# Decoder block on one core: later layernorm rows normalised on GpSimd, query parts in PSUM or on GpSimd, query stack loaded in two sets of heads

## The reference

```python
x = x + self_attention(layernorm(x))              # 16 heads of 64, softmax over the queries' axis
x = x + cross_attention(layernorm(x), ctx, mask)  # q = layernorm(x) @ Wq + bq, 16 heads of 8, 512 keys
x = x + ffn(layernorm(x))                         # softmax gate, best 2 of 8 experts, and a shared expert

def layernorm(x):
    return (x - mean(x)) / sqrt(var(x) + 1e-5)
```

## Time and profile before

| | us |
|---|---|
| median of 3 runs | 215.52 (213.54 to 216.35) |
| the profiled execution | 215.22 |
| its span, first to last instruction | 213.4 |
| PE busy | 198.2 (93%) |
| DVE busy | 160.9 (75%) |
| ACT busy | 131.9 (62%) |
| POOL busy | 91.2 (43%) |

### The profile page before, as it was taken

One profiled execution on the slowest core, in us unless ns is written; L12 is line 12 of the kernel. 1 busy time (PEld: TensorE's weight loads), 2 busy tenths in 40 slices (PEclk: granted clock), 3 DMA queues, 4 the chain that ended last, 5 costly groups with the idle time before them and its releaser, 6 DMA issues.

```text
span 213.4 us, 4411 instructions
## 1 busy us (share of the span) xinstructions
PE 198.2 (93%) x1562; PEld 153.6 (72%) x1562; DVE 160.9 (75%) x421; ACT 131.9 (62%) x308; POOL 91.2 (43%) x133
## 2 busy tenths in 40 slices
PE   7999998999799798697979999999898999999993
PEld 7788776777667575564646566566576899999993
DVE  2578688657659996379999999998994677458752
ACT  2465468669748838168868989988696532362320
POOL 7599017687456566604999700000120003611422
PEclk9999999999999999998899999999999999999999
DMA  6960748999546114024003300000000000000000
GB/s 169 386 172 3 197 49 99 121 108 109 60 57 178 65 30 107 15 60 166 0 0 96 54 3 0 2 3 2 0 3 0 5 0 3 0 0 28 0 0 25
DMA packets 10876, 12.67 MB, mean 59 GB/s; under 512 B 880, under 2 KB 8816, under 8 KB 10784
## 3 DMA queue, kind: packets, MB, share of 16 engines
q1 hardware_dynamic: 10040, 11.28, 26.5%
q10 hardware_dynamic: 720, 0.93, 1.3%
q0 software_dynamic: 96, 0.20, 0.5%
HBM read 10.96 MB, written 1.44 MB: 58 GB/s over the span
## 4 chain that ended last, share of the span: by engine, by line
PE 71%; DVE 17%; issue 5%; ACT 5%; POOL 1%; POOLq 0%; DVEq 0%; ACTq 0%
PE ps L897 12%; PE ps L858 9%; PE ps L918 7%; PE ps L835 6%; PE ps L785 6%; PE ps L674 5%; PE ps L801 5%; PE ps L817 5%; PE ps L757 4%; DVE q_t L1123 4%; PE ps L646 3%; PE ps L687 3%; DVE low L1113 3%; ACT prob L562 2%; PE ps L875 2%
## 5 line engine op out<-in xcount | busy, mean ns | idle before, releaser
L1123 DVE CUSTOM_DVE_ANT_0 q_t<-ps,mask_add 128x512 f32<-128x512 f32 x64 | 41.3, 683 | 5.3 <-PE ps L817 4.0
L457 POOL TENSOR_TENSOR prob<-prob,rec 128x512 f32<-128x512 f32 x32 | 32.7, 1049 | 28.3 <-DVE rec L1176 28.3
L562 ACT ACTIVATE prob<-ps,low 128x256 f32<-128x256 f32 x64 | 29.7, 490 | 11.7 <-DVE low L1113 11.7
L596 ACT ACTIVATE q_t<-q_t,low 128x512 f32<-128x512 f32 x44 | 29.3, 717 | 7.4 <-DVE low L1123 7.4
L392 POOL TENSOR_TENSOR rstd<-var_eps,minus_half 128x2 f32<-128x2 f32 (+1 forms) x5 | 3.9, 773 | 61.0 <-DVE var_eps L984 60.9
L858 PE MATMUL ps<-ident,q_t 128*128 128x128 f32 x176 | 24.1, 278 | 3.9 <-DVE place_o L1219 1.4
L858 PEld LDWEIGHTS ps<-ident,q_t 128*128 128x128 f32 x176 | 20.1, 143 | 10.1 <-issue 4.0
L1113 DVE TENSOR_REDUCE low<-ps 128x2 f32<-128x512 f32 x32 | 20.5, 681 | 7.9 <-PE ps L757 7.9
L582 ACT ACTIVATE q_t<-ps 128x512 f32<-128x512 f32 x18 | 10.6, 599 | 21.0 <-PE ps L897 21.0
L817 PE MATMUL ps<-k_stack,q_stack 72*128 72x512 bf16 x64 | 19.4, 390 | 1.8 <-issue 1.8
L801 PE MATMUL ps<-ident,prob 128*128 128x128 f32 x128 | 18.0, 278 | 2.1 <-DVE prob_t L1180 2.1
(11 more groups left out here) (166 smaller groups left out, 430.3 us busy)
## 6 DMA issues: line engine op xcount, KB each, us to landing
k_stack<-k_dram SPq DMA_DIRECT2D x9, 256.0 KB
q_stack<-q_dram SPq DMA_DIRECT2D x6, 192.0 KB
wg<-in_L_ffn_w_gate SPq DMA_DIRECT2D x1, 1024.0 KB, 24.8
wu<-in_L_ffn_w_up SPq DMA_DIRECT2D x1, 1024.0 KB, 36.1
k_dram<-prob SPq DMA_DIRECT2D x1, 768.0 KB, 3.6
w_in<-in_L_attn_Wq ACTq DMA_DIRECT2D x2, 256.0 KB, 5.6
context<-in_ctx SPq DMA_DIRECT2D x1, 512.0 KB, 5.8
w_in<-in_L_attn_Wv SPq DMA_DIRECT2D x1, 512.0 KB, 7.5
```

Source lines behind the costliest of these rows:

```text
L457: nc.gpsimd.tensor_tensor(pr, pr, rec1[:, s % 2, r, :].unsqueeze(2).to_broadcast([P, C, S]), ALU.mult).then_inc(s_norm1, 1)
L562: e = nc.scalar.activation(prob1[:, s % 3, r, c * S:(c + 1) * S], ps[:, 2 * (s % 2) + r, c * S:(c + 1) * S], ACT.Exp, bias=low1[:, s % 2, ...
L596: nc.scalar.activation(prob2[n % 3][:, c, :], score2[n % 2][:, c, :], ACT.Exp, bias=low2[:, n % 2, c:c + 1], scale=-1.0).then_inc(s_exp2, 1)
L1123: nc.vector.tensor_tensor_reduce(out=score2[n % 2][:, c, :], in0=ps[:, 2 * (n % 2) + c, :], in1=mask_add[:, c, :], scale=1.0, scalar=3e38, ...
```

## The change

- The rows of the four later layernorms (two batches, before cross attention and before the experts) are normalised on GpSimd: adding epsilon, the power and the two `tensor_scalar` operations stand there one behind the other (`normalise`), in the iteration of `residual` and ahead of that iteration's `divide1`. DVE keeps the statistics. The first layernorm stays on DVE.
- DVE makes batch 0's query parts in place in PSUM, and in g = 12 ahead of `reciprocals1(13)`. For batch 1 DVE only adds the bias and scales into SBUF, and GpSimd makes the parts (`split_queries2`) between two of its weight splits.
- The query stack of each batch is loaded in six DMAs: three with heads 0 to 3, then three with heads 4 to 15, and PE waits for each set where its first head comes.

```diff
+QSETS = ((0, 4), (4, H2))
...
-                for j in range(PARTS):
-                    r = j * PARTS * HD2
-                    load(q2_stack[r:r + PARTS * HD2, :, b * S:(b + 1) * S],
-                         q2_dram[b].rearrange("i (d h) t -> (i d) h t", d=HD2), d_qstack[b])
+                rows = q2_dram[b].rearrange("i (d h) t -> (i d) h t", d=HD2)
+                for i, (first, last) in enumerate(QSETS):
+                    for j in range(PARTS):
+                        r = j * PARTS * HD2
+                        load(q2_stack[r:r + PARTS * HD2, first:last, b * S:(b + 1) * S],
+                             rows[:, first:last, :], d_qstack[b][i])
...
+                if k >= 1:
+                    link(nc.gpsimd.tensor_scalar(var_eps[:, first:first + count], mean_var[:, first:first + count, 1],
+                                                 EPS, None, ALU.add))
...
+            def normalise(k, src, first):
+
+                link(reciprocal_std(k, first, C))
+                for c in range(first, first + C):
+                    ins = nc.gpsimd.tensor_scalar(x_hat[:, c, :], src[:, c, :], mean_var[:, c, 0:1],
+                                                  rstd[:, c:c + 1], ALU.subtract, ALU.mult)
+                ins.then_inc(s_xhat, 1)
...
+            def split_queries2():
+
+                pool.wait_ge(s_q2t, 1)
+                pool.wait_ge(d_qdram[0], 16)
+                link(nc.gpsimd.tensor_copy(q2_parts[:, 0, :], q2_t[:, :]))
+                link(nc.gpsimd.tensor_tensor(q2_rest[:, :], q2_t[:, :], q2_parts[:, 0, :], ALU.subtract))
+                link(nc.gpsimd.tensor_copy(q2_parts[:, 1, :], q2_rest[:, :]))
+                nc.gpsimd.tensor_tensor(q2_parts[:, 2, :], q2_rest[:, :], q2_parts[:, 1, :], ALU.subtract
+                                        ).then_inc(s_qparts, 1)
...
             for g in range(LAST_G + 2):
                 n = g - N_SELF
+                for kind, b, _ in BETWEEN.get(g, ()):
+                    if kind == "residual":
+                        normalise(1 + b, x1, b * C)
+                    elif kind == "residual2":
+                        normalise(3 + b, x2, b * C)
                 if g < N_SELF:
                     divide1(g)
...
-                if h == 0:
-                    pe.wait_ge(d_qstack[b], 16 * PARTS)
+                for i, (first, _) in enumerate(QSETS):
+                    if h == first:
+                        pe.wait_ge(d_qstack[b][i], 16 * PARTS)
...
+            def query_parts(b):
+
+                dve.wait_ge(s_q2ps, b + 1)
+                bank = ps[:, MID_BANK, S:2 * S]
+                if b == 1:
+                    nc.vector.tensor_scalar(q2_t[:, :], bank, bias2[:, 0:1], -SCALE2, ALU.add, ALU.mult
+                                            ).then_inc(s_q2t, 1)
+                    return
+                link(nc.vector.tensor_scalar(bank, bank, bias2[:, 0:1], -SCALE2, ALU.add, ALU.mult))
+                link(nc.vector.tensor_copy(q2_parts[:, 0, :], bank))
+                link(nc.vector.tensor_tensor(bank, bank, q2_parts[:, 0, :], ALU.subtract))
+                link(nc.vector.tensor_copy(q2_parts[:, 1, :], bank))
+                nc.vector.tensor_tensor(q2_parts[:, 2, :], bank, q2_parts[:, 1, :], ALU.subtract).then_inc(s_qparts, 1)
...
+                    for what in BETWEEN.get(g, ()):
+                        between(what)
                     reciprocals1(g + 1)
```

More of the change, by code:

```diff
@@ L63 @@
     11: [("residual", 0, 0)],
-    12: [("x_hat", 0, 0), ("turn", 0, 0), ("turned", 0, 0), ("q", 0, 0), ("parts", 0, 0)],
+    12: [("turn", 0, 0), ("turned", 0, 0), ("q", 0, 0), ("parts", 0, 0)],
     N_SELF + 3: [("residual", 1, 0)],
-    N_SELF + 4: [("x_hat", 1, 0)],
     N_SELF + 5: [("turn", 1, 0)],
@@ L74 @@
     N_SELF + 26: [("residual2", 0, 0)],
-    N_SELF + 27: [("x_hat2", 0, 0)],
     N_SELF + 28: [("turn2", 0, 0)],
@@ L293, in build @@
         d_qdram = [sem(f"d_qdram{b}") for b in range(B)]
-        d_qstack = [sem(f"d_qstack{b}") for b in range(B)]
+        d_qstack = [[sem(f"d_qstack{b}_{i}") for i in range(len(QSETS))] for b in range(B)]
         s_const, s_ident = map(sem, ("s_const", "s_ident"))
@@ L391, in reciprocal_std @@
                 pool.wait_ge(s_var, k + 1)
-                nc.gpsimd.tensor_tensor(rstd[:, first:first + count], var_eps[:, first:first + count],
-                                        minus_half[:, first:first + count], ALU.pow).then_inc(s_rstd, 1)
+                if k >= 1:
+                    link(nc.gpsimd.tensor_scalar(var_eps[:, first:first + count], mean_var[:, first:first + count, 1],
+                                                 EPS, None, ALU.add))
+                return nc.gpsimd.tensor_tensor(rstd[:, first:first + count], var_eps[:, first:first + count],
+                                               minus_half[:, first:first + count], ALU.pow)
+            def normalise(k, src, first):
[4 more added lines that the diff above has]
+                ins.then_inc(s_xhat, 1)
             nc.gpsimd.memset(v2[:, :, :, HD2 + 1:CW], 0.0)
@@ L469, in _ @@
                     if kind == "residual":
-                        reciprocal_std(1 + b, b * C, C)
                         add_bo2(b)
-                    elif kind == "residual2":
-                        reciprocal_std(3 + b, b * C, C)
                     elif kind == "turned2":
                         split_tokens(b)
+                    elif kind == "parts" and b == 1:
+                        split_queries2()
                 if 0 <= n - SPLIT_N < 2 * (NE + 1):
                     split_weights(n - SPLIT_N)
-            reciprocal_std(4, C, C)
             for i in range(N_FFN):
@@ L490, in _ @@
                     nc.gpsimd.tensor_tensor(sums, sums, y_part[k % 2], ALU.add).then_inc(s_acc, 1)
+                for kind, row, _ in FFN_BETWEEN.get(i + LAG_D, ()):
+                    if kind == "residual2":
+                        normalise(3 + row, x2, row * C)
         @block.scalar
@@ L985, in statistics @@
                                         EPS, None, ALU.add).then_inc(s_var, 1)
-            def normalise(k, src, first, count):
-                dve.wait_ge(s_rstd, k + 1)
+                dve.wait_ge(s_rstd, 1)
                 for c in range(first, first + count):
@@ L1191, in _ @@
                         low_scores1(g, r)
-                    for what in BETWEEN.get(g, ()):
-                        if what[0] == "x_hat":
-                            between(what)
                     low_scores1(g + 1, 0)
@@ L1213, in _ @@
                     probs_evac(g - 1, 1)
-                for what in BETWEEN.get(g, ()):
-                    if not (cycle(g) and what[0] == "x_hat"):
+                if not (cycle(g) and g < N_SELF):
+                    for what in BETWEEN.get(g, ()):
                         between(what)
```

18 lines of the change are left out of this document (5 added, 13 removed).

## The result

| | before | changed |
|---|---|---|
| median, us (4 runs each) | 214.97 (213.54 to 216.35) | 208.0 (207.6 to 208.76) |
| span of the profiled execution | 213.4 | 206.1 |
| PE, DVE, ACT, POOL busy | 198.2, 160.9, 131.9, 91.2 | 195.5, 153.2, 132.1, 100.2 |

The ratio is 0.968 (95% interval 0.961 to 0.975): 7.0 us less, where 5.3 were forecast. The ratios in this document leave out executions more than 1.5% above the fastest of their kernel; medians and ranges hold all of them.

The account below looks back on a forecast made before the run. PE was taken to set the end nearly everywhere. Terms 1.3 + 1.8 + 1.8 + 0.4 = 5.3 us off the profiled 215.22 gave 209.9, own range 208.8 to 211.0, whole range 207.5 to 213.0.

Parts of the forecast that it names:

- The wait before the first score: Between self and cross attention: loading queries in two sets hides PE's hole before the first cross score, 1.8 us.
- The entry without the hole: End of self attention: earlier, shorter query parts of batch 0 in PSUM let PE's transposes of pair 13 start earlier, 1.3 us.
- the bound of 0.73: Batch 0's layernorm on POOL: upper limit for one normalising operation, the time of a two-input operation twice as wide.
- Cost nothing, but the cover is thin: End of self attention: pair 11's divisions, queued behind POOL's layernorm, end at 72.8 instead of 69.76, still early enough.
- POOL is dear: Rival: normalising at 0.73 each and epsilon at 0.71 delay pair 11's divisions by 1.05 us; time 210.9, chance 0.10.
- the prediction's own sign: On POOL: the prediction is wrong if POOL's operations take over 0.8; normalising rows were expected at 0.4 to 0.5 each.
- The rule weighed in the prediction: DVE beside GpSimd: two SBUF inputs or a two-port mode wait; otherwise not. If wrong, 1.3 us delay stays, time 210.4.
- Cross attention: Cross attention, batch 1: DVE loses 3.5 us of work where it is full; PE gains 1.8 us, bounds 0 and 3.5.
- the argument that the engines meet each other soon: Cross attention: PE, DVE and ACT are nearly equally busy in the steady stretch, so only 0.4 of 1.3 us was counted.
- the upper bound: Cross attention, batch 1: PE gains at most the full 3.5 us that DVE loses there.
- The clock: Rival, cross attention: PE's clock may not fall, half of 1.7 us of PE time would show; time 209.1, chance 0.12.
- The later layernorms: After batch 0's first: DVE freed ahead of PE's wait at 150.10, 0.3, and in the expert steps, 0.1; together 0.4 us.

## Why the prediction was right, step by step

- **The wait before the first score, 1.8 us.** Right, mechanism and size: the sets alone gave 1.96. The first score came at 84.56 on the old clock (87.25 - 2.69), just outside the 84.0 to 84.5 forecast, and PE didn't wait for it. Not foreseen: the write to HBM took from 2.06 to 4.2 us, and two sets also covered that in the four profiles where it was late.
- **The entry without the hole, 1.3 us.** Half right. Measured 2.69 - 1.96 = 0.73. The step that failed is the price of a normalising operation on POOL: 0.80 us each, taken as 0.46, above even the bound of 0.73. Epsilon (0.25) and power (0.73) were right. So the divisions of pair 11 ended 6.08 us after the residual and not 5.2, 0.7 of these 0.85 by that price. PE waited for them, and the parts began 7.4 us after the residual, as before (7.5), not 6.6. PE's scores of pairs 14 and 15 began 9.03 us after it (75.45) where the working has 8.5, and that is nearly the whole 0.57 that is missing. "Cost nothing, but the cover is thin" was the sentence that broke. The rival "POOL is dear" happened in this term, by its normalising price and not by its epsilon. By the prediction's own sign (wrong if POOL's operations take over 0.8) it stands on the edge. The parts themselves took 2.3 us as worked out (2.35). Beside POOL's divisions the casts and subtractions with their inputs in SBUF took 0.99 to 1.15 us in the kernel before and in the four experiments that keep them there; only the first cast of the kernel before and of its version with two sets took 0.29, where one division ended and the next began. With their input, or one of two, in PSUM they took 0.42 to 0.43. The rule weighed in the prediction (the Trainium skill, SBUF — State Buffer, section Who interferes with whom) agrees with that.
- **Cross attention, 1.8 us.** Direction right, size too small: 3.21. The term counted the visible wait of 1.44 for the parts and 0.4 for the rest. Undone singly, the parts were worth 1.76 and the normalising 1.17; 2.9 of the 3.21 are these two; where the last 0.3 come from no run shows. What failed is the argument that the engines meet each other soon. It was read from the steady stretch, but the work was freed from the third head to the tenth, where in the kernel before DVE was nearly full and the others were not (columns as in the earlier trace rows):

```profile
94.30:112.33 18.03, 15.15 (x104) 9.80 (x103) 17.79 (x49) 14.37 (x25) 12.68 (x24) 0.91 0.20 66
```

  So nearly all came through of the 3.5 that were freed, which was the upper bound.
- **The clock.** It did not fall in the changed kernel, but this was no part of the gain: with and without a fall, cross took 60.69 on the old code. The rival had half of the 1.7 us come back; nothing did.
- **The later layernorms, 0.4 us.** Measured 0.25.
- **The sum.** 2.69 + 3.21 + 0.25 = 6.15 against 5.3: an error of 0.6 one way and 1.4 the other. The remaining 1.15 of the 7.3 between the two profiles lies ahead of the first edit. The medians are 7.0 apart; by the profiles' stretches 6.2 of that is the change, and the rest can be chance in a kernel whose executions range over 2.8 us and more. That the sum of the stretches came out within 0.9 of the forecast is in part luck: the term that was too large and the one that was too small have opposite signs.

## What to carry to other kernels

The visible wait need not be all that relief of the engine behind it is worth: here 1.44 us of wait stood for 3.2 of gain. Where an engine is full for eight iterations on end, put the upper bound at all the time that is freed there, and look in that stretch itself for the next engine's load. Before moving work to an engine, ask what is queued behind it there, and get the price of exactly that form of instruction: a form with two per-row scalars cost nearly twice an addition of the same size. A load that ends just in time should be cut so that its first piece is there early: the first piece also covered the late writes of this case. And before an operation is moved next to another engine's work, look at how the two overlap: a different place in the list was worth as much here as a different memory.

## What the runs showed of the hardware

- A GpSimd `tensor_scalar` of 128x128 with mean and reciprocal deviation as per-row scalars takes 0.79 to 0.81 us in all eight places; on two columns with a constant 0.23 to 0.25. The Trainium skill, GPSIMD Engine Reference, section Engine selection, calls operations with one input about line rate; a cast of 128x256 at 0.40 us agrees, this form does not.
- A write of 192 KB to HBM let SP go on 2.07 us after its issue (2.06 to 2.08) in nine profiles and 3.55 to 4.23 us after it in five. What made it late was not tested.
- PE's clock fell to 1.2 GHz after a hole of 3.4 us, and also within 96 to 104 us of an execution without a hole at the entry. Executions of that same kernel ran with a fall (mean 0.992) and without (1.000). What set it off was not found.
- Ahead of one and the same matmul of an out projection PE stood for 1.08, 1.17 and 2.57 us in three of fourteen profiles, with nothing that released it. Its cause was not tested and stays open.
